# V for all heads in a phase of its own, with seven quadrant products for eight, ahead of fused attention and a ternary FFN

## The reference, cut to what matters

```python
q, k, v = proj(x, Wq), proj(x, Wk), proj(x, Wv)        # y = x @ W.T, split into 16 heads of 64
q = q * min(cond, 4)
scores = q @ k.T / 8;  scores = where(causal, scores, min)
out = softmax(scores) @ v;  out = merge_heads(out) @ Wo.T
qx = round(out / s).clip(-128, 127) * s,   s = max(absmax(out), eps) / 127   # per token
qw = round(W / alpha).clip(-1, 1) * alpha, alpha = mean(|W|)
return x + qx @ qw.T + bias
```

## Time and profile before

| | |
|---|---|
| median of 3 runs | 2063.09 us (2062.89 to 2063.57) |
| the profiled execution | 2063.89 us, span 2062.1 us |
| PE busy | 2035.6 us, 99% of the span, 11747 matmuls |
| DVE, ACT, POOL busy | 1274.7 us (62%), 1010.7 us (49%), 803.8 us (39%) |
| TensorE clock granted | 0.999 of full speed |
| DMA | 194.51 MB, 94 GB/s over the span |

### The profile page before, as it was taken

One profiled execution on the slowest core, in us unless ns is written; L12 is line 12 of the kernel. 1 busy time (PEld: TensorE's weight loads), 2 busy tenths in 40 slices (PEclk: granted clock), 3 DMA queues, 4 the chain that ended last, 5 costly groups with the idle time before them and its releaser, 6 DMA issues.

```text
span 2062.1 us, 36378 instructions
## 1 busy us (share of the span) xinstructions
PE 2035.6 (99%) x11747; PEld 1725.0 (84%) x11778; DVE 1274.7 (62%) x3163; ACT 1010.7 (49%) x2383; POOL 803.8 (39%) x746
## 2 busy tenths in 40 slices
PE   8999999999999999999999999999999999999998
PEld 7888888888888888888888888888887777777775
DVE  5666666766666667666666766667766545455454
ACT  5656556655656566666565766656565000000000
POOL 3433333433333334344433433333334544444441
PEclk9999999999999999999999999999999999999999
DMA  4222223222222242222224223323223432333322
GB/s 164 72 73 89 92 71 138 77 78 72 71 72 71 79 140 72 72 71 71 72 89 155 73 98 115 121 93 93 92 72 104 137 122 92 112 101 104 109 98 75
DMA packets 85936, 194.51 MB, mean 94 GB/s; under 512 B 7392, under 2 KB 40160, under 8 KB 84320
## 3 DMA queue, kind: packets, MB, share of 16 engines
q1 hardware_dynamic: 85856, 193.50, 29.3%
HBM read 126.36 MB, written 33.55 MB: 78 GB/s over the span
## 4 chain that ended last, share of the span: by engine, by line
PE 48%; issue 30%; POOL 19%; ACT 1%; DVE 1%; POOLq 1%; DMA 0%; DVEq 0%; SPq 0%; ACTq 0%
PE proj_ps L170 18%; POOL prob L284 12%; PE s_ps L563 9%; PE proj_ps L563 8%; POOL parts L374 7%; PE o_ps L634 5%; PE t_ps L294 3%; PE o_ps L330 2%; PE s_ps L254 1%; PE s_ps L253 1%; PE t_ps L612 1%; ACT parts L370 0%; POOLq L283 0%; DMA w_raw<-wq 0%; ACT v_st L201 0%
## 5 line engine op out<-in xcount | busy, mean ns | idle before, releaser
L170 PE MATMUL proj_ps<-parts 128*128 128x512 f32 (+1 forms) x6144 | 1214.3, 345 | 10.1 <-DVE parts L374 10.1
L170 PEld LDWEIGHTS proj_ps<-parts 128*128 128x128 f32 x6144 | 929.9, 190 | 119.5 <-issue 10.1
L284 POOL TENSOR_TENSOR prob<-prob,row_inv 128x128 f32<-128x128 f32 (+3 forms) x512 | 393.4, 771 | 932.3 <-DVE row_inv L278 929.9
L265 DVE CUSTOM_DVE_ANT_0 prob<-s_ps,mask 128x128 f32<-128x128 f32 (+3 forms) x512 | 249.8, 488 | 340.3 <-PE t_ps L294 194.3
L308 ACT ACTIVATE pt_hi<-t_ps 128x128 fp32r<-128x128 f32 (+3 forms) x512 | 222.3, 434 | 434.7 <-PE t_ps L294 430.4
L272 ACT ACTIVATE prob<-prob,row_min 128x128 f32<-128x128 f32 (+3 forms) x512 | 286.3, 559 | 72.9 <-DVE row_min L265 66.9
L315 DVE TENSOR_TENSOR pt_lo<-t_ps,pt_hi 128x128 fp32r<-128x128 f32 (+3 forms) x512 | 249.5, 487 | 65.5 <-ACT pt_hi L308 59.9
L619 ACT ACTIVATE yt_q<-t_ps 128x1024 bf16<-128x1024 bf16 x32 | 32.8, 1025 | 428.0 <-PE t_ps L612 428.0
L294 PE MATMUL t_ps<-ident,prob 128*128 128x128 f32 x1280 | 227.7, 276 | 7.3 <-POOL prob L284 5.7
L374 POOL TENSOR_TENSOR parts<-x_raw,parts 128x512 fp32r<-128x512 f32 x128 | 203.1, 1607 | 51.5 <-ACT parts L370 51.5
L563 PE MATMUL proj_ps<-parts 128*128 128x512 f32 x768 | 186.2, 396 | 0.0
(11 more groups left out here) (65 smaller groups left out, 1902.9 us busy)
## 6 DMA issues: line engine op xcount, KB each, us to landing
x_raw<-xT SPq DMA_DIRECT2D x128, 512.0 KB, 5.5
k_sw<-k_st SPq DMA_DIRECT2D x128, 256.0 KB, 3.7
oT_scratch<-o_sum SPq DMA_DIRECT2D x64, 256.0 KB, 2.3
x_raw<-oT_scratch SPq DMA_DIRECT2D x32, 512.0 KB, 4.6
x_tile<-x SPq DMA_DIRECT2D x32, 512.0 KB, 5.2
out<-res SPq DMA_DIRECT2D x32, 512.0 KB, 3.1
w_raw<-wf SPq DMA_DIRECT2D x16, 512.0 KB, 5.6
w_raw<-wq SPq DMA_DIRECT2D x4, 1024.0 KB, 7.0
```

What stands on the lines that cost most here:

```text
L170: mm = pe.matmul(out, l, r, start=(k == 0 and i == 0), stop=(k == KT - 1 and i == 2))
L265: dve.tensor_tensor_reduce(prob[:, u % 4, 0:w], s_ps[u % 2][:, 0:w], mask[:, S - w:S], 1.0, -MASKED, ALU.add, ALU.min, row_min[:, u % 4:u ...
L284: pool.tensor_tensor(prob[:, u % 4, 0:w], prob[:, u % 4, 0:w], row_inv[:, u % 4:u % 4 + 1].broadcast_to([P, w]), ALU.mult).then_inc(norm_d ...
```

## The change

V leaves the steps. A new phase ahead of them (`v_sp`, `v_pe`, `v_act`, `v_dve`, `v_pool`) computes V of all 16 heads for all batches and writes it, already in high and low parts, to a DRAM scratch `v_scratch`; each step loads the V of its four heads back, one DMA of 256 KB for each head (`load_v`), and `times_v` waits for that DMA instead of for the evacuation.

The phase works on 16 pairs of 128-token tiles. A pair's product is a 2 by 2 block product: two token tiles by two halves of the output features, over two halves of the contraction. Pair 0 is done plainly (96 matmuls of 512 columns) while the weights arrive. Pairs 1 to 15 use seven products of sums and differences of quadrants instead of eight products (84 matmuls of 512 columns each). The sums are made once for the weights (`wv_sums`, DVE) and once for each pair for x (`xv_sums`, POOL), each sum being split in parts like any operand; three result sums are made on DVE (`v_sum`) and one on POOL (`v_ur`).

The steps are rewritten without the V groups. NPROJ falls from 8 to 4, and the 32 slices J that are left are spread over the 16 units, mostly two between one S and the next. The boundary between steps moves: a step now starts with S(5) of the units before it, where it started with S(8).

```diff
+    v_scr = nc.dram_tensor("v_scratch", (B, QT, P, NG, HG, 2 * DH), F32, kind="Internal").ap()
-        groups = [("q", 0), ("k", 0), ("q", 1), ("k", 1)] + [("v", t) for t in range(QT)]
-        EVAC = [2, 4, 6, 8, 9, 10, 11, 12]
+        groups = [("q", 0), ("k", 0), ("q", 1), ("k", 1)]
+        EVAC = [2, 4, 6, 8]
         def times_v(pe, it, h):
-            if h == 0:
-                pe.wait_ge(const_ready, 4)
-                pe.wait_ge(proj_lo_done, (it + 1) * NEV)
+            pe.wait_ge(v_in[h], (it + 1) * 16)
+        def load_v(sp, it, g, b, h):
+            if due(count := it * HG - HG + h + 1):
+                sp.wait_ge(pv_done, count)
+            sp.dma_start(v_st[:, :, h, :].bitcast(F32), v_scr[...]).then_inc(v_in[h], 16)
+        def wv_sums(dve):
+            a11, a12, a21, a22 = wv_quad(0, 0), wv_quad(0, 1), wv_quad(1, 0), wv_quad(1, 1)
+            dve.wait_ge(wv_lo_done, 2 * KT)
+            dve.tensor_tensor(a22, a21, a22, ALU.add).then_inc(wv_sum_done, 1)
...
+        def v_product(pe, n, c):
...
+            for k in range(CH):
+                for m, (xp, wp) in enumerate(((1, 0), (0, 1), (0, 0))):
+                    mm = pe.matmul(bank[:, :], xv[:, c, xp, ks], wv_view(c, wp)[:, k, :], ...)
+        def v_pe(pe):
+            v_plain(pe)
+            for n in range(1, PAIRS):
+                v_product(pe, n, A11)
+                v_product(pe, n, S4)
+                v_product(pe, n, A12)
+                v_product(pe, n, S2)
+                v_product(pe, n, S1)
+                v_product(pe, n, S3)
+                v_product(pe, n, A22)
+        def v_pool(pool):
+            xv_sums(pool, 1)
+            ws_low(pool, S2)
+            ws_low(pool, S3)
+            for n in range(1, PAIRS):
+                xv_sums(pool, n + 1)
+                v_ur(pool, n)
         def act_step(...):
...
+            H(15)
+            E(1)
+            X(0, 1)
+            W(2)
+            H(0)
+            E(2)
+            X(2, 3)
```

More of the change, by code:

```diff
@@ L676, in pairs @@
                     body(i * 2 + p, p)
+        PAIRS = TILES // 2
+        V_LAST = 7 * (PAIRS - 2)
+        A11, S4, A12, S2, S1, S3, A22 = range(7)
+        B11, B22, B21, T2, T1, T3, T4 = range(7)
+        A21_PLAIN = S3
+        B_PLAIN = [[T2, T1], [T3, T4]]
+        V_PIECES = [(0, 1), (1, 2), (2, 4), (4, 6), (6, 8)]
+        xv_in = [sem(f"xv_in{i}") for i in range(2)]
+        wv_in = [sem(f"wv_in{i}") for i in range(len(V_PIECES))]
+        wv_hi_done = sem("wv_hi_done")
+        wv_lo_done = sem("wv_lo_done")
@@ new lines, in wv_split @@
+        def wv_split(eng, k, low):
+            for i, c in enumerate((A11, A21_PLAIN) if k < CH else (A12, A22)):
+                raw = wv_raw[:, k, i * HALF:(i + 1) * HALF]
+                if low:
+                    eng.wait_ge(wv_hi_done, 2 * k + i + 1)
+                    eng.tensor_tensor(wv_view(c, 1)[:, k % CH, :], raw, wv_view(c, 0)[:, k % CH, :].bitcast(F32),
+                                      ALU.subtract).then_inc(wv_lo_done, 1)
+                else:
+                    eng.activation(wv_view(c, 0)[:, k % CH, :], raw, ACT.Copy).then_inc(wv_hi_done, 1)
@@ new lines, in v_plain @@
+        def v_plain(pe):
+            for k in range(KT):
+                pe.wait_ge(wv_lo_done, 2 * k + 2)
+                if k % CH == 0:
+                    pe.wait_ge(xv_lo_done, 2 * (k // CH) + 2)
+                ks = slice(k % CH * P, (k % CH + 1) * P)
+                for j in range(2):
+                    c = B_PLAIN[k // CH][j]
+                    for i, a in enumerate((A11, A21_PLAIN) if k < CH else (A12, A22)):
+                        for m, (xp, wp) in enumerate(((1, 0), (0, 1), (0, 0))):
+                            mm = pe.matmul(plain_bank(j, i)[:, :], xv[:, c, xp, ks], wv_view(a, wp)[:, k % CH, :],
+                                           start=(k == 0 and m == 0), stop=(k == KT - 1 and m == 2))
+                        if k == KT - 1:
+                            mm.then_inc(v_plain_done, 1)
@@ L1025, in dve_step @@
             I(13)
+            W(0)
             M(14)
@@ L1126, in sp_step @@
                 load_o(sp, 1, 1)
+                load_wo(sp, 0)
+                load_wo(sp, 1)
             if ending:
+                load_wo(sp, 3)
+            if now:
+                load_v(sp, *now, 0)
+                load_v(sp, *now, 1)
+            if wf_part == 1:
+                load_wf(sp, 4)
+                load_wf(sp, 5)
+            if wf_part == 2:
+                load_wf(sp, KT)
+                load_wf(sp, KT + 1)
+            if ending:
+                load_wo(sp, 4)
+                load_wo(sp, 5)
                 load_wo(sp, 6)
@@ L1157, in sp_step @@
                 load_wf(sp, KT + 2 * wf_part - 1)
[L1158 to L1163 removed]
+        CONSTS = 2 + 3 + 3
         block = ctx.enter_context(nc.Block())
```

889 lines of the change are left out of this document (568 added, 321 removed).

## The result

The changed kernel takes 2135.61 us (median of 4 runs, 2134.66 to 2138.99) beside 2063.33 us for the kernel before on the same chip (4 runs, 2062.89 to 2064.62): a ratio of 1.035, 95% interval 1.0334 to 1.0370, or +72 us. The forecast was 2099 (+36) in a range of 2030 to 2138. The sign and the wide range held; the forecast's own range of 2075 to 2120 did not, and half of the loss was missed.

The account below looks back on a forecast made before the run. It took PE, busy for 99% of the span, as the bound. The terms -57.9 - 1.1 + 8 + 2 + 60 + 9 + 12 + 4 = +36.0 gave 2099 us, range 2030 to 2138, the forecast's own 2075 to 2120.

Parts of the forecast that it names:

- V's own work: On PE: 3072 matmuls of 256 columns removed, 1356 of 512 added at 0.238 us each: -57.9 us.
- the prediction's own signs of being wrong: Loop step under 37.4 us, PE waiting at S or in the phase's pairs, or 512-column matmuls not 0.238 there.
- The start and the phase's one-off waits: Phase of V: first matmul at 10.8, net -1.1 us; waits for POOL's sums, R's copy and first `v_ur`, +8.
- The hand-over: From phase to steps: first S(0) waits for K's swap with five slices of cover instead of eleven, +2 us.
- What a step needs without waits: PE in a step keeps 22.8 us of Q and K, loses 11.9 of V, and needs 36.4.
- The lateness, 2.0 a step x 30: S(0) to S(8): PE waits at T for N, late by 2.0 us a step, bounds 0 and 3.2: +60.
- W splits: Three times W splits, 1.27 us each on DVE, fall into the S(0) to S(8) half: +3 each, +9.
- `wf` steps: Four steps where Q adds 4.1 us to DVE, both lots in the full half: +3 each, +12.
- The ending: Carries units 5 to 15 instead of 8 to 15, six Wo splits instead of four, first Y waits earlier: +4.
- DVE and ACT become the bound: Rival, as in the ending: steps lose 3.2 us instead of 2.0, +36 more, 2135 us; 13%.
- the new order holds: Rival: DVE's and ACT's lateness is absorbed to 0.3 us a step, -30, 2033 us; 25%.
- K's swap comes late each step: Rival: swap late by 0.5 to 1.5 us a step, PE waiting at S, 2115 to 2140 us; 7%.

Follow-up runs that it names:

- The gap-free step: Changed kernel with T(0), T(3), T(4), T(5) one slice later, T(1) behind PV(3), two transfers mended, x splits on 8 of 512 columns from the second step: 2038.8 us.
- a later Y: YY(0) and YY(1) moved behind PV(0) in the ending, on the changed kernel with T's moved later and two transfers mended: 2104.2 us.
- The run with x tiny: Changed kernel with each split of x handling 8 of 512 columns from the second step on, waits and order kept: 2071.8 us.
- the later T's: Changed kernel with T(0), T(3), T(4), T(5) one slice J later on PE and T(1) behind PV(3): 2117.4 us, step 38.95.
- the other mends: Changed kernel with K's first swap issued ahead of loads of x and V, and absolute sums of `wf` later on ACT: alone 2122.7 us.
- the old order without V: Changed kernel's phase kept, steps in the order of the kernel before with V taken out: 2303.6 us.
- the storing steps: First group's steps store x's parts in DRAM, 24 others load them; on the changed kernel with T's moved later and two transfers mended: 2131.0 us.

## Why the prediction was right in sign and half in size

- **V's own work**: mis-sized, in the change's favour. A matmul of 512 columns in the phase takes 0.227 us, not 0.238: 12 in 2.72, as these two rows show.

```profile
153.14 2.88 PE L868 MATMUL o_ps<-wv_first,xv 128*128 128x512 f32 x12
155.86 2.88 PE L868 MATMUL t_ps<-wv_last,xv 128*128 128x512 f32 x12
```

  1356 x 0.2267 = 307.4 for 322.7: 15.3 better. The 0.238 came from a run of nine that changes to S; in steps six still take 1.47, 0.245 each. Both are 0.1 us for the change on top of 0.2267 a matmul. That a matmul in the phase is not 0.238 was one of the prediction's own signs of being wrong. The Trainium skill's 215.7 ns (TensorE: Matmul & The Clock Gate, "Wait — 56ns, not 53.3ns?") isn't reached in long runs either.
- **The start and the phase's one-off waits** (net -1.1 and +8): the first matmul came at 14.18, not 10.8, and the phase lost 14.0 us beyond its matmuls, not 8. POOL's weight parts were late once, as forecast (2.64), but the largest wait was a sum on DVE (4.68), and the clock fell behind both (below). Phase end 335.6 for about 342: 15.3 less for V, 9.4 more for these; the hand-over's miss of 6 uses up the rest, so that the first S(0) came when it was forecast. That is luck.
- **The hand-over** (+2): failed. It's 8.72 of wait (8.2 in the sum below), 6 of it the queue: the swap is issued at 349.96 behind stores of V and loads of x and V. The prediction counted slices of cover and left out what SP had in front.
- **What a step needs without waits** (-11.9): right. The gap-free step measures 36.88; 48.73 - 11.9 = 36.83.
- **The lateness, 2.0 a step x 30**: the mechanism right, the size not: 39.63 - 36.88 = 2.75 in all 31 steps, 85 for 60. This is the step that failed most, by 25 of the 35 us. It followed the units with mean lengths, once from a clean start. T(0), T(1) and T(5) came out nearly as said (0.25, 0.75, 0.88 for 0.2, 0.6, 0.9); T(3), put 0.2 late, was on time; T(4) was 0.67 late for 0.1. The walk has V(3) on ACT, but not V(3) and L(2) on DVE ahead of I(4), where the rows above have I(4) at 810.81 with E(4) done at 810.27. Moved waits reappeared just there, at T(3) to T(5).
- **W splits** (+9): too dear, +1.0 each, 3 in all. **`wf` steps** (+12): four at +3.1 to +3.8, 13 together, near the forecast; and 6.0 more in one where ACT waits for a load: 19 in all.
- **The ending** (+4): failed: 9.3, since V's 11.9 left it, four slices (2.8) came, and it takes as long as before. It waits 3.84 ahead of the first Y, 0.5 to 2.2 at five T's and 1.7 at a PV; a later Y didn't mend it. The sum had no term for the loads of Wo: ACT, ahead of E of the units, waits 6.2 us for them in all, 4.08 at once, where it waited 0.8 before. What an earlier load would give, no run shows.
- **The rival "DVE and ACT become the bound"** named 2135 us, the time measured, and the wide range holds the time only because it reaches out to there. That is luck: its 3.2 us a step are 2.75, V's own work and the W splits came out cheaper, and the phase, the hand-over, the load of `wf` and the ending came out dearer.
- **The rival "the new order holds"** asked for under 1.07 us a step. The run with x tiny (37.82, waits 0.9) sits there, at 2071.8 with the one-off losses in it. The rival that K's swap comes late each step did not happen in the change, but did as soon as more transfers stood ahead of it.

The sum again, with measured terms: -380.6 + 307.4 + 2.3 (start: 14.18 - 10.11, less the 1.8 of starvation that goes) + 14.0 (phase) + 8.2 (hand-over, what the +329.2 leaves, with the 2.8 that moved) + 85 + 3 + 19 + 9.3 = +67.6. The traces differ by 70.6. The 3 us that are left lie in the steps, about half of them in the first: before it was 2.0 shorter than the others (46.71 us; no T(14), T(15) and PV(3) in it), after only 0.5 (39.10), and 1.0 of that went when K's swap came earlier.

## What to carry to other kernels

Taking work off the bound engine makes room only if the others' work fits the shorter step in every half of it, not on average (DVE at 79% and ACT at 76% of PE's time looked harmless, and cost 2.75 us a step): measure it first, by making the covered work tiny, which here gave 37.82 a step in the first run and, with the later T's, both the floor (36.88) and what a full solution may win (26 us, with the other mends in). If one late instruction is moved and the wait reappears two units on, stop reordering and remove work. For one-off hand-overs, and for weights loaded late in a kernel, read the queue that issues the transfer, not only the slices that cover it, and take the length of a step from one instruction to its own repeat.

## What the runs showed of the hardware

**The clock after a wait.** Before, the granted clock was 0.999. After, it was 0.992, and the losses follow PE's idle stretches. Windows as above: twelve matmuls in a full stream; the twelve behind the 2.64 wait; the stretch with the 4.68 wait; the twelve behind it.

```profile
37.71:40.43 2.72, 2.72 (x14) 2.25 (x12) 2.72 (x2) 2.72 (x4) 2.58 (x2) 1.00 0.00 0
48.67:53.00 4.33, 4.33 (x12) 3.25 (x12) 4.33 (x2) 1.05 (x3) 4.33 (x1) 0.63 0.00 0
53.00:57.84 4.84, 0.15 (x2) 0.03 (x1) 4.84 (x8) 0.00 (x0) 1.81 (x2) 0.74 0.36 144
57.84:62.65 4.81, 4.81 (x13) 3.82 (x13) 2.92 (x3) 1.75 (x3) 4.52 (x4) 0.56 1.04 285
```

At 0.56 most of that stretch ran at the lower of the two levels, 1.2 GHz, and the twelve took 4.81 for 2.72. A wait of 2.64 thus cost 1.6 more behind it, one of 4.68 another 2.1; the hand-over and the ending show the same (0.91 and 0.93 in the windows at the top), and behind the 8.72 wait the clock stays at 0.50 for 5.75 us:

```profile
360.15:365.90 5.75, 5.75 (x16) 4.69 (x17) 2.45 (x8) 2.52 (x7) 0.40 (x1) 0.50 0.10 24
```

The 0.3 to 0.9 us waits at T cost nothing of this kind: 1.00 in every regular step. In the old order without V, where T(2), T(3) and T(5) start 1.1 to 1.8 us late, it is 0.944 over the whole span: there the lower clock comes on top of the waits.

**Transfers queue.** Swaps of 256 KB that landed 3.7 us after issue held PE up for 1.8 to 2.5 us at the end of six of the storing steps and 6.5 at worst once loads and stores of megabytes were issued ahead of them, with the DMA engines at 0.57 of their time, not full, from 700 to 936 us.
